# Four-layer graph network, one core: last pair columns split between two paths, a later clear, weights prepared earlier, one vector product per output tile

## The chip, the cores and the metric

The kernel runs on one core of a Trainium2 chip. The metric is the device time of one execution, in microseconds. The core has five engines that run their own instruction streams and wait for each other with semaphores: TensorE (PE, matrix products into PSUM), VectorE (DVE), ScalarE (ACT, activations and copies), GpSimd (POOL, here mostly indirect DMAs) and SyncE (SP, DMAs).

## What is computed

N = 1250 nodes with D = 512 features, E = 40000 edges sorted by `dst`. Four layers, each added to `x` and normalised by row. The first three need sums over edges, which the kernel writes as products with dense adjacency matrices; the last one (a SchNet-like filter network) needs an own product for every edge. Cut to what matters:

```python
def residual_norm(x, f):                  # _layernorm(x + f(x)), eps 1e-5
    y = x + f; return (y - mean(y)) / sqrt(var(y) + eps)
# L0: h = x + segment_sum(x[src], dst);  relu(h @ W1 + b1) @ W2 + b2
# L1: twice: relu(h @ W_self + (segment_sum(h[src], dst) / max(deg, 1)) @ W_neigh + b)
# L2: relu(segment_sum((x @ W)[src] * edge_weight[:, None], dst) + bias)
# L3: idx_i = src, idx_j = dst, f_ij = edge_attr_20, rcut_ij = edge_weight, r_ij = edge_attr_3
xs = x[:, :C] @ (W_in2f_s / sqrt(C));  xv = einsum('nci,cf->nfi', x[:, C:], W_in2f_v) / sqrt(C)
h = shifted_softplus(f_ij @ Wf1 + bf1)
W = (h @ Wf2 + bf2) * rcut_ij[:, None]    # the filter of each edge
agg = segment_sum(messages(xs[idx_j], xv[idx_j], W, r_ij), idx_i)   # 8 blocks of 128 used
S = shifted_softplus(agg[:, :2*F] @ (W1_s / sqrt(2*F))) @ (W2_s / sqrt(C))
V = einsum('nmi,mc->nci', agg[:, 2*F:8*F].reshape(n, 2*F, 3), W1_v) / sqrt(2*F)
V = einsum('nci,cd->ndi', V, W2_v) / sqrt(C)
```

## The kernel before

**Stages, in order.** Each engine has one program written out in order; nothing is scheduled by a planner. The nodes are NT = 10 row tiles of 128 (the last has 98 rows). The edges are 125 partitions by EJ = 320 columns, in BLOCKS_J = 10 blocks of LJ = 32 columns.

1. *Sorting the edges by pair of tiles (0 to 387 us).* Every edge gets a place in a table of (source tile, target tile) pairs (PAIR), and later one in a table sorted by source tile (SRC). `places` and `split_places` on DVE compute the places from products of PE. Then the pair records reach the table on two paths. The columns of the blocks in `DMA_BLOCKS` (six of ten, 192 columns, `DMA_COLS`) are written to DRAM by POOL, one indirect DMA for each column (L529), and the whole table is read back at the end (`pair_sb`, SP L438, after `pair_scat`). The columns of the other four blocks (128, `PERM_COLS`) go through TensorE: `one_hots` on DVE (L1307 to L1311) and `scale` on ACT (L1031) make five one-hot operands of a column, and `permute` on PE (L744) adds five products into PSUM, which I call one column product. A ring of four operand sets joins the three engines. PE runs some column products between other work; what is left when the input layer `x_up` is done runs as one backlog, all but the last LAST = 16 of it before DVE clears a part of the adjacency area (L1400, L1321) and the last 16 behind that. At the end DVE clears one more piece (L1405) and adds the PSUM sums to the table that was read back (L1412).
2. *Adjacency matrices (387 to 695 us)*: 416 chunks, `blocks` on PE (L800, L801), added by DVE (L1432). At its end POOL starts the 320 columns of the SRC table (L543).
3. *Layers L0, L1, L2 (695 to 1273 us)*: dense products on PE. The last is `l2_agg`, whose ten tiles DVE turns into the new `x` (`residual`, L1468 to L1459) as they come.
4. *The way into L3 (1273 to 1304 us)*: PE transposes `x` (`l3_xT`, L856), multiplies it (`l3_z`, L863), ACT copies each tile (L1090) and stores it to DRAM in `z_table` (L1092, on ACT's own queue, behind a wait for the copy). DVE prepares the weights of L3 (L1548 to L1585) behind its last `residual` tile. POOL clears the sums `agg` (L618, 128 x 10240), splits the edge attributes of two groups (`split`, L571 to L577), and then gathers rows of `z_table` for four chunks (L594), before it makes the low half of the hidden layer (`hidden_lo`, L602). ACT loads its table of functions (L1170).
5. *The edge loop of L3 (1304 to 2234 us)*: 322 chunks of 128 edges in 93 groups.
6. *The end (2234 to 2284 us)*: for each row tile PE transposes the sums (`sums_T`, L961), multiplies them with the first weights (`mixed`: L970 for the scalar part, L972 for the vector part), and after an activation with the second ones (`outputs`, four products, L982). ACT copies the transposed sums (L1193), copies the vector part (L1205) and computes the softplus (L1207 to L1209). DVE finishes the softplus (`activated`, L1667), adds `x` (L1673, L1675) and takes mean and variance (L1677, L1678) in `finish`. After the last tile come one square root for all rows (ACT L1211), a reciprocal (L1687), ten normalisations on DVE (L1691) and ten stores on ACT's queue (L1214).

Memory is reused all the time: `agg` lies where the adjacency matrices were, so it can't be cleared before the last `l2_agg` product has read them; `identb`, an operand of `attrs_T` (L875), lies there too.

## Time and profile before

| | us |
|---|---|
| median of 3 runs | 2282.49 (2280.95 to 2283.18) |
| the profiled execution | 2285.5, its span 2283.7 |
| PE busy | 2048.1 (90% of the span) |
| DVE busy | 1549.3 (68%) |
| POOL busy | 1393.4 (61%) |
| ACT busy | 1122.1 (49%) |

The chain that ended last is 68% PE, 10% DVE and 10% POOL. So PE sets the pace on the whole, but not in every stage: the POOL part is all in the first 387 us, and the DVE and ACT parts are at the borders between stages. A share of busy time is an average over all of them; what an edit is worth is read in its own stage.

### The profile page before, as it was taken

The page shows a single profiled execution, that of the slowest core. Times are in us where ns is not written, and L with a number is a line of the kernel's source. Part 1 is how long each engine was busy: PE and PEld are TensorE (multiplying, and loading weights), DVE is VectorE, ACT ScalarE, POOL GpSimd, SP SyncE. Part 2 cuts the span into 40 slices and gives each one's busy share as a digit, 9 for nine tenths or more (in the row PEclk, how much of TensorE's full clock was granted, in tenths as well). Part 3 has the DMA queues.
Part 4 walks back from the last instruction along what each step waited for, and adds up shares of the span by engine and source line. Part 5 has one row for each costly group of instructions (what it writes and reads, how often), then busy time and mean ns, then how long its engine had stood idle before and what let it go on. Part 6 is the DMA issues. An engine that isn't in the chain of part 4 may idle for free.

```text
span 2283.7 us, 37069 instructions
## 1 busy us (share of the span) xinstructions
PE 2048.1 (90%) x7761; PEld 1159.7 (51%) x7761; DVE 1549.3 (68%) x4326; ACT 1122.1 (49%) x3234; POOL 1393.4 (61%) x1718
## 2 busy tenths in 40 slices
PE   4788794777889999999999799999999999999986
PEld 3444342555665555455444555555555555555545
DVE  8987666888885251111403588888888888888885
ACT  0476454777771010000010466666666666666654
POOL 1477886444446888888885466666666666666530
PEclk9698797777779999999999899999999999999999
DMA  5410321000002121121120233333333333333321
GB/s 193 158 16 3 88 69 17 0 0 0 0 0 65 39 44 20 21 62 20 29 54 12 78 98 98 98 100 100 99 100 98 98 98 98 99 99 101 93 67 46
DMA packets 75080, 147.01 MB, mean 64 GB/s; under 512 B 26829, under 2 KB 37570, under 8 KB 74631
## 3 DMA queue, kind: packets, MB, share of 16 engines
q0 software_dynamic: 44704, 95.66, 17.3%
q1 hardware_dynamic: 27356, 45.20, 6.0%
q10 hardware_dynamic: 2946, 5.28, 0.6%
q8 instruction: 33, 0.54, 0.1%
q14 instruction: 41, 0.34, 0.0%
HBM read 123.11 MB, written 22.40 MB: 64 GB/s over the span
## 4 chain that ended last, share of the span: by engine, by line
PE 68%; DVE 10%; POOL 10%; issue 7%; DMA 2%; DVEq 2%; ACT 2%; ACTq 0%; SPq 0%; POOLq 0%
PE ps L910 24%; PE ps L653 11%; POOL pair_table L529 10%; PE ps L672 9%; PE ps L848 4%; PE ps L893 3%; PE ps L895 3%; PE ps L894 3%; PE ps L896 3%; DVE adj_t L1432 2%; PE ps L801 2%; DVE adj_t L1232 1%; DVE dense L1418 1%; DVE dense L1419 1%; DMA pair_table<-dense 1%
## 5 line engine op out<-in xcount | busy, mean ns | idle before, releaser
L910 PE MATMUL ps<-adj_t 128*128 128x512 f32 x1288 | 615.2, 600 | 14.3 <-DVE adj_t L1641 14.3
L1124 ACT ACTIVATE adj_t<-adj_t 128x128 f32<-128x128 f32 x966 | 315.3, 389 | 211.6 <-DVE adj_t L1620 189.4
L594 POOL DMA_INDIRECT adj_t<-z_table,adj_t x322 | 313.3, 973 | 154.5 <-DVE adj_t L1630 68.5
L910 PEld LDWEIGHTS ps<-adj_t 128*128 128x128 f32 x1288 | 231.2, 189 | 249.8 <-issue 215.6
L529 POOL DMA_INDIRECT pair_table<-dense x192 | 236.2, 1230 | 131.2 <-issue 120.7
L543 POOL DMA_INDIRECT src_table<-st_two,src_rows x216 | 262.9, 1217 | 70.5 <-issue 65.2
L801 PE MATMUL ps<-dense 128*128 128x128 f32 x832 | 226.7, 385 | 0.0
L672 PE MATMUL ps<-wring,dense 128*128 128x512 f32 (+1 forms) x480 | 209.9, 599 | 4.6 <-issue 3.9
L1432 DVE TENSOR_TENSOR adj_t<-adj_t,ps 128x256 f32 x416 | 173.5, 417 | 53.4 <-PE ps L801 40.6
L893 PE MATMUL ps<-dense_r 128*128 128x512 f32 x322 | 200.3, 622 | 2.3 <-POOL dense_r L602 2.3
L602 POOL TENSOR_TENSOR dense_r<-adj_t,dense_r 128x512 fp32r<-128x512 f32 x81 | 104.6, 1291 | 156.1 <-ACT dense_r L1133 155.9
L800 PE MATMUL ps<-dense 128*128 128x128 bf16 x416 | 109.0, 262 | 84.6 <-ACT dense L1059 75.8
L1622 DVE TENSOR_TENSOR adj_t<-adj_t,ps 128x384 f32<-128x384 f32 x322 | 176.0, 547 | 0.0
L801 PEld LDWEIGHTS ps<-dense 128*128 128x128 f32 x832 | 174.6, 260 | 1.6
L555 POOL TENSOR_SCALAR dense<-iotab,dense 128x128 bf16<-128x128 bf16 x104 | 68.5, 658 | 173.9 <-PE ps L801 165.1
L653 PE MATMUL ps<-adj_t,xa 128*128 128x512 f32 (+1 forms) x480 | 170.0, 516 | 3.6 <-DVE adj_t L1432 3.6
L1058 ACT ACTIVATE dense<-dense 128x128 f32<-128x128 bf16 x416 | 126.8, 305 | 88.3 <-DVE dense L1419 75.3
L1059 ACT ACTIVATE dense<-dense 128x128 f32<-128x128 bf16 x416 | 160.4, 386 | 0.0
L1641 DVE TENSOR_TENSOR adj_t<-adj_t,ps 128x1024 f32 x93 | 113.6, 1221 | 62.0 <-PE ps L910 61.0
L1620 DVE TENSOR_TENSOR adj_t<-adj_t,ps 128x256 f32<-128x256 f32 x322 | 133.7, 415 | 30.4 <-PE ps L896 27.7
L744 PE MATMUL ps<-dense 125*128 125x416 bf16 x640 | 143.3, 368 | 10.7 <-ACT dense L1031 10.3
L672 PEld LDWEIGHTS ps<-wring,dense 128*128 128x128 f32 (+1 forms) x480 | 90.8, 190 | 121.5 <-issue 121.5
(276 smaller groups left out, 3835.1 us busy)
## 6 DMA issues: line engine op xcount, KB each, us to landing
src_table<-dense SPq DMA_DIRECT2D x8, 656.0 KB, 6.6
adj_t<-z_table,adj_t POOLq DMA_INDIRECT x322, 3.5
records<-dense SPq DMA_DIRECT2D x1, 5000.0 KB
adj_t<-src_table SPq DMA_DIRECT2D x73, 64.0 KB
adj_t<-zeros SPq DMA_DIRECT2D x1, 4576.0 KB
src_table<-st_two,src_rows POOLq DMA_INDIRECT x216
st_two<-records POOLq DMA_DIRECT2D x54, 62.5 KB
adj_t<-zeros SPq DMA_DIRECT2D x1, 3328.0 KB
```

The costliest lines, as they stand in the source:

```text
L529: g.indirect_dma_start(out=pair_table, out_offset=bass.IndirectOffsetOnAxis(ap=rows_i[PAIR][0:EP, j:j + 1].bitcast(u32), axis=0), in_=pair ...
L543: g.indirect_dma_start(out=src_table, out_offset=bass.IndirectOffsetOnAxis(ap=rows_i[SRC][0:EP, j:j + 1].bitcast(u32), axis=0), in_=st_rec ...
L594: g.indirect_dma_start(out=zg[:, s, c, :], out_offset=None, in_=z_table, in_offset=bass.IndirectOffsetOnAxis(ap=dsti[:, s, c:c + 1].bitcas ...
L653: last = mm(b[:, 0:w], feats[:, t, m * P:(m + 1) * P], adj[:, k_of, t * N + c0:t * N + c0 + w], start=t == 0, stop=t == NT - 1)
L672: last = mm(b[0:r, :], lhs[:, k, t * P:t * P + r], w[:, k, :], start=a == 0 and k == 0, stop=a == len(parts) - 1 and k == KT - 1)
L801: mm(bank[c][:, P:2 * P], sel_f[:, c, 0, :], sel_f[:, c, 1, :], start=True, stop=True).then_inc(blk_done, 1)
L893: mm(bW[c], h_hi[:, s, e], wf2_hi, start=True, stop=False)
L910: last = mm(bank[6 + h], oh[:, c, :], msg[:, c, h * D:(h + 1) * D], start=c == c0, stop=c == c0 + count - 1)
L1059: A(sel_f[:, c, 1, :], sel_b[:, c, 1, :], ACT.Copy, scale=dense[:, ds(n * PAIR_COLS + (PAIR_AT + 2), 1)]).then_inc(selw_ready, 1)
L1124: last = A(msg[:, c, (2 + k) * P:(3 + k) * P], msg[:, c, MSG:MSG + P], ACT.Copy, scale=side[:, s, c, C_Y - ATT + k:C_Y - ATT + k + 1])
L1432: v.tensor_tensor(a, a, bank[c][:, 0:2 * P].rearrange("p (k n) -> p k n", k=2), ALU.add).then_inc(blk_added, 1)
L1622: v.tensor_tensor(msg[:, c, 5 * P:8 * P].rearrange("p (a n) -> p a n", a=3), zg[:, s, c, P:4 * P].rearrange("p (a n) -> p a n", a=3), b[:, ...
```

## The change

Five things, all in the order of the engines' programs:

- **Pair columns.** The last block of columns (block 9, `SHARED`) is cut in two: 16 of its columns stay with the DMAs, 16 become column products. So POOL issues 176 indirect DMAs and not 192, and PE, ACT and DVE make 144 column products and not 128. `split_places` does both kinds of work for that block.
- **The way into L3.** POOL's clear of `agg` waits for the last `residual` tile, not for the last `l2_agg` product. DVE prepares the L3 weights before the `residual` tiles of `l2_agg`; only `identb` and one small clear stay behind them. SP stores the z tiles, not ACT. ACT loads its table before the z copies. Only two gathers stand ahead of the first `hidden_lo`, and two behind it.
- **The vector weights.** Two new products make W1_v times W2_v once, before the loop: PE transposes `w1v`, ACT copies it, PE multiplies it with W2_v, ACT copies the result over `w1v`.
- **The end, vector part.** `mixed` writes the vector part of the output directly, with six 128 x 128 products for a tile (the L972 products and three of the four L982 products go away), and ACT's copy L1205 goes away.
- **The end, normalisation.** Each tile is normalised and stored (by SP) as soon as it can be. For tiles 0 to 7 ACT makes a first guess of the inverse root with Ln and Exp, and POOL refines it with four small instructions; for the last two ACT takes the square root and DVE the reciprocal.

```diff
-DMA_COLS = [t * LJ + c for t in DMA_BLOCKS for c in range(LJ)]
-PERM_COLS = [j for j in range(EJ) if j // LJ not in DMA_BLOCKS]
+SHARED = BLOCKS_J - 1
+DMA_COLS = [t * LJ + c for t in DMA_BLOCKS for c in range(LJ // 2 if t == SHARED else LJ)]
+PERM_COLS = [j for j in range(EJ) if j not in DMA_COLS]
...
@@ SP
             load_group(0, 0)
             load_group(0, 1)
+            for t in range(NT):
+                sp_eng.wait_ge(done["l3_z"], t + 1)
+                sp_eng.dma_start(z_table[t * P:t * P + rows_of(t), :], xb[0:rows_of(t), t, :]).then_inc(z_out, 16)
...
+            for t in range(NT):
+                sp_eng.wait_ge(y_ready, t + 1)
+                sp_eng.dma_start(out[t * P:t * P + rows_of(t), :], xa[0:rows_of(t), t, :]).then_inc(out_done, 16)
...
@@ POOL
-            pool.wait_ge(full, first["l2_agg"] + NT)
+            pool.wait_ge(done["l2_agg"], NT)
             g.memset(agg, 0.0).then_inc(agg_zero, 1)
             split(0, 0)
             split(0, 1)
-            for c in range(GROUP):
-                gather(0, 0, c)
+            gather(0, 0, 0)
+            gather(0, 0, 1)
             hidden_lo(0, 0)
+            gather(0, 0, 2)
+            gather(0, 0, 3)
...
+            for t in range(NT - 2):
+                pool.wait_ge(guessed, t + 1)
+                r, w = rstd[:, t:t + 1], rtmp[:, t:t + 1]
+                link(g.tensor_tensor(w, r, r, ALU.mult))
+                link(g.tensor_tensor(w, w, stat[:, 1, t:t + 1], ALU.mult))
+                link(g.tensor_scalar(w, w, -0.5, 1.5, ALU.mult, ALU.add))
+                g.tensor_tensor(r, r, w, ALU.mult).then_inc(refined, 1)
...
@@ PE
             pe.wait_ge(l3w_ready, 2)
+            for k in range(2):
+                last = nc.tensor.transpose(bank[6][:, k * P:(k + 1) * P], w1v[:, k, :], ident[:, :])
+            last.then_inc(wT_done, 1)
             for s in range(2):
                 attrs_T(0, s)
                 filter_in(0, s)
+            pe.wait_ge(wT_copied, 1)
+            for k in range(2):
+                last = mm(bank[7][:, k * P:(k + 1) * P], w1vT[:, k, :], w2sv[:, 1, :], start=True, stop=True)
+            last.then_inc(w12_done, 1)
+            pe.wait_ge(w12_ready, 1)
             filter_out(0, 0, 0)
...
@@ PE, mixed and outputs
-                for k in range(2):
-                    last = mm(svbank[s][:, P:D], w1v[:, k, :], aT[:, s, 2 + 3 * k:5 + 3 * k, :].rearrange("p m n -> p (m n)"),
-                              start=k == 0, stop=k == 1)
                 last.then_inc(sv_done, 1)
+                if t >= 2:
+                    pe.wait_ge(o_read, t - 1)
+                for m in range(3):
+                    for k in range(2):
+                        last = mm(obank[s][:, (1 + m) * P:(2 + m) * P], aT[:, s, 2 + 3 * k + m, :], w1v[:, k, :], start=k == 0, stop=k == 1)
+                last.then_inc(v_done, 1)
...
-                for m in range(KT):
-                    last = mm(obank[s][:, m * P:(m + 1) * P], svT[:, s, m * P:(m + 1) * P], w2sv[:, 0 if m == 0 else 1, :], start=True, stop=True)
-                last.then_inc(o_done, 1)
+                mm(obank[s][:, 0:P], svT[:, s, :], w2sv[:, 0, :], start=True, stop=True).then_inc(o_done, 1)
...
@@ ACT
             copies_T("l3_xT")
+            nc.scalar.preload_act_table_set("natural_log_exp_and_others")
...
-                act.wait_ge(done["l3_z"], t + 1)
-                act.dma_start(z_table[t * P:t * P + r, :], xb[0:r, t, :]).then_inc(z_out, 16)
...
+            act.wait_ge(wT_done, 1)
+            A(w1vT, bank[6][:, 0:2 * P].rearrange("p (k n) -> p k n", k=2), ACT.Copy).then_inc(wT_copied, 1)
             attrs(0, 0)
             softplus_exp(0, 0)
             softplus_log(0, 0)
             attrs(0, 1)
+            act.wait_ge(w12_done, 1)
+            A(w1v, bank[7][:, 0:2 * P].rearrange("p (k n) -> p k n", k=2), ACT.Copy).then_inc(w12_ready, 1)
             hidden_hi(0, 0)
...
@@ ACT, the end
+            def root(t):
+                r = rows_of(t)
+                act.wait_ge(var_ready, 3 * NT + t + 1)
+                if t < NT - 2:
+                    link(A(rstd[0:r, t:t + 1], stat[0:r, 1, t:t + 1], ACT.Ln))
+                    A(rstd[0:r, t:t + 1], rstd[0:r, t:t + 1], ACT.Exp, scale=-0.5).then_inc(guessed, 1)
+                else:
+                    A(rstd[0:r, t:t + 1], stat[0:r, 1, t:t + 1], ACT.Sqrt).then_inc(std_ready, 1)
...
-                A(svT[:, s, P:D], sv[:, P:D], ACT.Copy).then_inc(act_sv, 1)
...
@@ DVE
-            residual("l2_agg", 64, relu=True)
...
-            link(v.tensor_copy(identb, ident[:, :]))
...
+            residual("l2_agg", 64, relu=True)
+            link(v.tensor_copy(identb, ident[:, :]))
             v.memset(stat, 1.0).then_inc(l3w_ready, 1)
...
@@ DVE, the end
+                v.tensor_scalar(stat[0:r, 1, t:t + 1], stat[0:r, 1, t:t + 1], EPS, None, ALU.add).then_inc(var_ready, 1)
+
+            def normalised(t):
+                r = rows_of(t)
+                y = xa[0:r, t, :]
+                if t < NT - 2:
+                    dve.wait_ge(refined, t + 1)
+                else:
+                    dve.wait_ge(std_ready, 3 * NT + t - (NT - 2) + 1)
+                    link(v.reciprocal(rstd[0:r, t:t + 1], rstd[0:r, t:t + 1]))
+                v.tensor_scalar(y, y, stat[0:r, 0, t:t + 1], rstd[0:r, t:t + 1], ALU.subtract, ALU.mult).then_inc(y_ready, 1)
...
                 finish(t)
...
+                if t:
+                    normalised(t - 1)
+            normalised(NT - 1)
```

What the diff doesn't show is where the work then stands on an engine. On PE, at the end of the first stage (`wring,adj_t` is the input layer, `ps<-dense` with 416 columns a fifth of a column product), before:

```order
L744 MATMUL ps<-dense 128x416 x5
L756 MATMUL ps<-ident,xa 128x98 x4
L744 MATMUL ps<-dense 128x416 x5
L767 MATMUL ps<-wring,adj_t 128x512 x4
L744 MATMUL ps<-dense 128x416 x10
L767 MATMUL ps<-wring,adj_t 98x512 x4
L744 MATMUL ps<-dense 128x416 x125
```

and now:

```order
L765 MATMUL ps<-dense 128x416 x5
L777 MATMUL ps<-ident,xa 128x98 x4
L765 MATMUL ps<-dense 128x416 x5
L788 MATMUL ps<-wring,adj_t 128x512 x4
L765 MATMUL ps<-dense 128x416 x10
L788 MATMUL ps<-wring,adj_t 98x512 x4
L765 MATMUL ps<-dense 128x416 x205
```

The column products between other work are the same; the backlog behind the input layer grows from 25 to 41.

On ACT, between the last z copy and the first hidden layer, before:

```order
L1090 ACTIVATE dense<-ps 98x512
L1092 DMA z_table<-dense 98x512
L1170 ACT_TABLE_LOAD
L1100 ACTIVATE adj_t<-ps 126x512
L1108 ACTIVATE adj_t<-ps 128x512
L1110 ACTIVATE adj_t<-adj_t 128x512
L1116 ACTIVATE adj_t<-adj_t,wring 128x512
L1100 ACTIVATE adj_t<-ps 126x512
L1133 ACTIVATE dense_r<-adj_t 128x512
```

and now:

```order
L1116 ACT_TABLE_LOAD
L1119 ACTIVATE dense<-ps 128x512 x9
L1119 ACTIVATE dense<-ps 98x512
L1198 ACTIVATE adj_t<-ps 128x256
L1127 ACTIVATE adj_t<-ps 126x512
L1135 ACTIVATE adj_t<-ps 128x512
L1137 ACTIVATE adj_t<-adj_t 128x512
L1143 ACTIVATE adj_t<-adj_t,wring 128x512
L1127 ACTIVATE adj_t<-ps 126x512
L1204 ACTIVATE wring<-ps 128x256
L1160 ACTIVATE dense_r<-adj_t 128x512
```

The stores and the table load are gone from between; the two copies of 128x256 (L1198, L1204) are new, and the second stands ahead of `hidden_hi` (L1160, before L1133).

On PE, one tile of the end, before:

```order
L961 MATMUL ps<-ident,adj_t 128x128 x8
L970 MATMUL ps<-adj_t,wring 128x128 x2
L972 MATMUL ps<-adj_t,wring 128x384 x2
L982 MATMUL ps<-wring,dense 128x128 x4
L961 MATMUL ps<-ident,adj_t 128x128 x8
```

and now:

```order
L990 MATMUL ps<-ident,adj_t 128x128 x8
L999 MATMUL ps<-adj_t,wring 128x128 x2
L1005 MATMUL ps<-wring,adj_t 128x128 x6
L1011 MATMUL ps<-wring,dense 128x128
L990 MATMUL ps<-ident,adj_t 128x128 x8
```

And on DVE, one tile of the end, before:

```order
L1667 SCALAR_TENSOR_TENSOR dense<-ps,adj_t 128x128
L1673 TENSOR_TENSOR xa<-ps,xa 128x128
L1675 TENSOR_TENSOR xa<-ps,xa 128x3x128
L1677 BN_STATS lnt<-xa 128x6
L1678 BN_AGGR ybuf<-lnt 128x2
```

and now:

```order
L1706 SCALAR_TENSOR_TENSOR dense<-ps,adj_t 128x128
L1712 TENSOR_TENSOR xa<-ps,xa 128x128
L1714 TENSOR_TENSOR xa<-ps,xa 128x3x128
L1716 BN_STATS lnt<-xa 128x6
L1717 BN_AGGR ybuf<-lnt 128x2
L1718 TENSOR_SCALAR ybuf<-ybuf 128x1
L1728 TENSOR_SCALAR xa<-xa,ybuf,dense 128x512
```

PE loses two long and three short products for six short ones; DVE gains two instructions, one of them as wide as a tile.

## Rows read from the trace of the kernel before

**Rows 1.** Chain that ended last, 378 to 390 us: start, us, what.
```profile
378.03 1.19 POOL pair_table L529
...
379.52 2.61 DMA pair_table<-dense
...
386.85 2.50 DVE dense L1412 x3
```

**Rows 2.** PE, 320 to 392 us: start, us, instructions, idle before and its releaser.
```profile
350.52 15.59 PE L744 MATMUL ps<-dense 125*128 125x416 bf16 x80 [9.32 <-ACT dense L1031]
```

**Rows 3.** L744 alone: length, PE busy (x), PEld busy (x), granted clock, DMA.
```profile
196.90:201.40 4.50, 3.63 (x10) 1.17 (x10) 0.50 0.11 8
...
355.00:366.00 11.00, 11.00 (x64) 5.97 (x61) 1.00 0.09 4
```

**Rows 4.** DVE, 350 to 392 us, columns as in Rows 2.
```profile
366.52 1.42 DVE L1405 MEMSET adj_t<- 128x1632 f32 x1 [2.58 <-PE ps L744]
```

**Rows 5.** DVE, 1170 to 1315 us.
```profile
1265.00 0.55 DVE L1459 TENSOR_SCALAR xa<-ybuf,lnt 128x512 f32<-128x512 f32 x1
1270.57 0.69 DVE L1468 TENSOR_TENSOR ybuf<-ps,shared 98x512 f32<-98x512 f32 x1 [5.02 <-PE ps L848]
...
1273.59 5.85 DVE L1459 TENSOR_SCALAR xa<-ybuf,lnt 98x512 f32<-98x512 f32 x1
...
1299.88 0.69 DVE L1595 SCALAR_TENSOR_TENSOR adj_t<-ps,adj_t 128x512 f32<-128x512 f32 x1 [9.63 <-ACT adj_t L1116]
```

**Rows 6.** POOL, 1170 to 1315 us.
```profile
1270.53 8.64 POOL L618 MEMSET adj_t<- 128x10240 f32 x1 [35.93 <-PE ps L848]
...
1283.33 0.19 POOL L588 CAST adj_t<-adj_t 128x4 int32<-128x4 f32 x1
1297.34 1.03 POOL L594 DMA_INDIRECT adj_t<-z_table,adj_t  x1 [13.82 <-DMA z_table<-dense]
...
1302.18 1.28 POOL L602 TENSOR_TENSOR dense_r<-adj_t,dense_r 128x512 fp32r<-128x512 f32 x1
```

**Rows 7.** PE, 1170 to 1315 us.
```profile
1279.50 2.62 PE L856 MATMUL ps<-ident,xa 128*128 128x128 f32 x12 [5.90 <-DVE xa L1459]
1281.91 10.65 PE L863 MATMUL ps<-wring,dense 128*128 128x128 f32 x80
...
1303.61 0.77 PE L893 MATMUL ps<-dense_r 128*128 128x512 f32 x1 [2.31 <-POOL dense_r L602]
```

**Rows 8.** PE alone: length, PE busy (x), granted clock, DMA.
```profile
1279.50:1284.00 4.50, 4.50 (x22) 0.50 0.00 0
```

**Rows 9.** Chain that ended last, 1293 to 1298 us: start, us, what.
```profile
1294.16 0.61 ACT dense L1090
...
1294.79 2.28 DMA z_table<-dense
```

**Rows 10.** ACT, 1170 to 1315 us.
```profile
1295.16 1.28 ACT L1170 ACT_TABLE_LOAD   x1 [0.40 <-ACT dense L1090]
```

**Rows 11.** PE, 2190 to 2284 us: one tile of the end.
```profile
2255.45 1.04 PE L961 MATMUL ps<-ident,adj_t 128*128 128x128 f32 x8
...
2256.77 1.46 PE L972 MATMUL ps<-adj_t,wring 128*128 128x384 f32 x4
2258.06 1.05 PE L982 MATMUL ps<-wring,dense 128*128 128x128 f32 x8
2258.95 1.04 PE L961 MATMUL ps<-ident,adj_t 128*128 128x128 f32 x8
```

**Rows 12.** DVE, 2190 to 2284 us.
```profile
2256.29 0.29 DVE L1667 SCALAR_TENSOR_TENSOR dense<-ps,adj_t 128x128 f32<-128x128 f32 x1 [1.31 <-ACT adj_t L1209]
...
2258.27 0.18 DVE L1678 BATCH_NORM_AGGREGATE ybuf<-lnt 128x2 f32<-128x6 f32 x1
...
2273.37 0.18 DVE L1678 BATCH_NORM_AGGREGATE ybuf<-lnt 98x2 f32<-98x6 f32 x1
```

**Rows 13.** ACT's DMA issues, 2274 to 2284 us.
```profile
2274.87 5.88 ACTq L1214 DMA_DIRECT2D out_x<-xa  x10
```

47 lines of the change are left out of this document (21 added, 26 removed).

## The prediction, made before the changed kernel was run

> **What bounds the kernel now.** I read the chain that ended last first, since it says for each stage which engine's end was waited for, and then the instructions in order of time at the borders between stages, since all edits lie there. The long dense products (695 to 1273 us) and the edge loop (1304 to 2234 us) are PE's and are not touched. Three places are.
>
> *The front, up to 387 us.* The reader sees in [rows 1] that the chain runs through POOL: the last indirect DMA starts at 379.52, 1.49 behind the one before, has landed at 382.13, and once the table has been read back DVE adds the sums at 386.85. The other path is done long before: PE's column products end at 366.11 [rows 2], DVE's last clear at 367.94 [rows 4]. So POOL's path is 18.9 us later than PE's.
>
> *The way into L3.* At 1273.59 DVE's normalisation of the last tile takes 5.85 us where the tile before took 0.55 [rows 5]. It ends at 1279.44; POOL's clear, 8.64 us from 1270.53, ends at 1279.17 [rows 6]. PE stands still for 5.90 us, released by that instruction [rows 7], and its granted clock then is 0.50, the lower of its two levels, until 1284 [rows 8]. The first gather waits until the last z tile has been stored, 1297.07 [rows 6, 9], and the first filter product until POOL has made the low half, 1303.61 [rows 6, 7].
>
> *The end.* PE is busy without a gap: a tile takes 3.50 us (2255.45 to 2258.95), of which 1.32 are transposes and scalar product, 1.29 the long vector products, 0.89 the four output products [rows 11]. From DVE's last statistics (2273.55 [rows 12]) to the end of the span, 2283.7, come another 10.15 us: root, ten normalisations and ten stores, whose issue ends at 2280.75, 2.95 before the end [rows 13].
>
> **The change part by part.** The sums are made against the profiled execution (2285.5, span 2283.7). It is 3.0 above the median of the runs; I carry the difference over to the median.
>
> *Front.* POOL saves 16 DMAs at 1.49 us, 23.9 us: its last issue and the read-back are that much earlier, so DVE could add the sums at 363. The other path gets 16 more column products, all of them in the backlog behind the input layer, where nothing hides them. A product's price: at full clock 64 fifths take 11.0 us, 0.86 us a product [rows 3]; in the whole last run, with its slow start, 80 take 15.59, 0.97 us [rows 2]. I take 0.92, in the middle, since the slow start is there only once: 14.8 us, between 13.8 and 15.6. The products end at 380.9; DVE's clear starts 0.41 behind them as now and takes 1.42 [rows 4]; the sums are added at 382.7 in place of 386.85. **Gain 4.1 us**, 3.3 to 5.1. What is late next is PE's path itself, so each us on it counts from now on. The three extra small instructions of `split_places` I cost at nothing, since DVE then waits for PE's bases of the source tables; uncovered they are 1 us.
>
> *The way into L3.* With the clear behind the last `residual`, the normalisation takes 0.55 and PE goes on at 1274.25. The weight preparation, 10.8 us (from 1279.44 to 9.63 before 1299.88 [rows 5]), now runs while PE works on `l2_agg`; DVE waits 5.02 us for PE before a tile there [rows 5], so it has caught up after two or three tiles: nothing. PE: twelve transposes take 2.62 at clock 0.50 [rows 7, 8] and half of that, 1.3, at full clock, which there is no pause to take away. A z tile then costs what eight records of the same shape cost in the end stage, 0.89 [rows 11], ten of them 8.9 in place of 10.65 [rows 7]. PE ends at 1284.6. ACT's copies (0.61 [rows 9]) follow PE without stores between them; the table load (1.28 [rows 10]) lies in the wait for the first z tile. Last copy done at 1285.2, stored 2.28 later at 1287.5, gather 0.28 behind, at 1287.8. POOL: clear from 1274.25 to 1282.9, then two splits and small copies, 4.35 as before (1279.17 to 1283.52 [rows 6]): ready at 1287.3. So the gather comes 9.5 earlier, and POOL, only 0.5 behind the store, is late next.
>
> The hidden layer's path: `attrs_T` starts 0.3 after the last copy, behind two transposes of w1v, at 1285.5. Before, it followed the last copy (1294.77) too, but ACT's next step stood behind the table load until 1296.44, some 0.8 longer than it had to [rows 9, 10]. So the hidden layer is ready about 1290.3 in place of 1300.57 [rows 5]. Now ACT's `hidden_hi` stands behind the copy of the combined weights, and that behind the second `filter_in`, which waits for the hidden layer itself: 0.7 for this product (0.77 for one as wide at half clock, L893 [rows 7]), 0.4 to 0.9 for two products of four records (0.11 each [rows 11], twice that at half clock), 0.4 to 0.6 for the copy. No row has this wait; the least is 0, if the copy falls into a pause, the most 2.5. I take 2.0, near the sum of its links. Then 0.6 for `hidden_hi`, POOL's low half (1.28 [rows 6]) from 1292.9 to 1294.2, and the first filter product at 1294.3 in place of 1303.61. **Gain 9.3 us**, 6 to 11.5. The two gathers moved behind the low half are issued by 1296.8 and needed by DVE about 1300. Loop and dense stages stay as they are.
>
> The 5.85 us have a rule of the Trainium skill beside them: SBUF — State Buffer, section Who interferes with whom, says that VectorE and GpSimd share a pair of ports as a lock, and whoever starts first holds it for its whole instruction. By that rule the cast of `identb`, now right behind the last `residual`, may wait for the clear to end at 1282.9; PE asks for it at 1285.3, so it would delay nothing, with 2.4 us to spare.
>
> *The end.* PE: six short products at 0.22 (0.89/4 [rows 11]) cost 1.34 for the 1.29 of the long ones, and one output product in place of four saves 0.67: 2.88 us a tile, 0.62 less. DVE: a tile's work from L1667 to the end of L1678 is 2.16 us [rows 12]; it gains the sum with epsilon (about as long as L1678, 0.2) and a normalisation (0.55 [rows 5]), with their starts 3.0. So DVE becomes the bound, at about 3.05 us a tile. Following both engines tile by tile with these prices (for the old order this gives the traced 2273.55), the last statistics come 3.1 us earlier. Then root, reciprocal and small steps, 0.77 (2273.55 to the first normalisation, which ends where the first store is issued, 2274.87 [rows 12, 13]), the last normalisation 0.55, 0.2 for tile 8's in between, an issue of 0.6 (5.88/10), and a landing between 1.9 (the z store behind its own issue) and 2.95: 4.5 us in place of 10.15. Together 8.7. From it I take 0.5 for DVE held up by POOL's four small instructions a tile; no row shows that pair, the bounds are 0 and 3 us. **Gain 8.2 us**, 5.5 to 9.5.
>
> *Sum*: 4.1 + 9.3 + 8.2 = 21.6. The profiled execution would take 2263.9, the median 2282.5 - 21.6 = **2261 us**.
>
> **The rivals.**
>
> *A, POOL holds the way into L3*: the splits run slower beside DVE, or the combined weights cost more, and only the stalled 5.3 us come back; the end gives 5.5. 4.1 + 5.3 + 5.5 = 14.9: 2267.6. For it: POOL is 0.5 us from being the bound, and DVE takes work in both places. Against: the same splits took 4.35 beside a busy DVE.
>
> *B, the front gives nothing*: at 1.18 us a column product (18.9/16) PE's path is as late as POOL's was: 2265. For it: ACT and DVE feed each product, beside POOL's DMAs. Against: 0.86 to 0.97 so far.
>
> *C, slower: the backlog at the lower clock.* At granted clock 0.50 two products hold 3.63 us, 1.73 to 1.82 each [rows 3]. The backlog is 41 long; it starts at 333 (nine products of 0.9 before the pause that begins at 341.2 [rows 2]), holds that pause of 9.3 and ends 1.8 before the sums: they are added at 344 + 41p. With the other gains of 17.5 the kernel is slower than before once 344 + 41p passes 404.4, from 1.47 us a product on. At 1.73 the sums come 28 late: 2293. For it: the clock does fall in this stage. Against: 1.00 from 355 to 366, once PE was busy.
>
> *D, another chain is as late*, and within 0.2% comes out, 2280. For it only that the chain shows one path of several; against it three plain waits of 18.9, 5.9 and 10.15 us, each on the chain.
>
> *E, more*: 2253, with free combined weights and a short landing.
>
> **How the numbers follow.** The forecast has 0.58, A 0.18, B 0.12, E 0.05, D 0.04, C 0.03. The likeliest is 2261. Its terms' bounds give gains of 14.8 to 26.1, so 2256 to 2268, with A and B inside; I widen to 2254 and 2270, which leaves D, C and part of E out. 0.2% is 4.6 us, about what a measurement of this kernel can tell from no change. Faster by more: forecast, A, B and E, 0.93, of which I give 0.01 away: 0.92. Within: D, 0.04. Slower: C and 0.01 unnamed, 0.04.
>
> **What would show it.** Front: the last indirect DMA at 355 to 357 us, the column products ending at 380 to 382, the sums added within 2.5 us of that; wrong if they come after 384, C if the products' run shows clock 0.50. Way into L3: the last normalisation 0.55, a pause of PE under 1 us, clock 1.00 through the z tiles, the gather 13 to 14 us after PE resumes and the first filter product 20 us after it (24.1 before). End: a tile every 3.05 us, DVE without pauses and PE with some, and 4.5 us from the last statistics to the end. The prediction is wrong if DVE waits there for POOL or ACT, or if the loop, which I leave alone, grows.

## The result, and the profile after

The changed kernel takes 2246.4 us in the median of four runs (2246.0 to 2248.2), where the kernel before, timed beside it, takes 2282.7. The ratio is 0.984, with a 95% interval of 0.983 to 0.986. That is 36 us faster; the forecast was 21.6, and 2246.4 lies below its range (2254 to 2270). The two profiled executions differ by about as much: spans of 2283.7 and 2246.0 us, 37.7 apart. Two of the runs that were timed later fell far outside all others, one of the kernel before at 4051.6 us and one of the changed kernel at 2672.6, and no ratio below holds them.

The span is cut into five stretches at the same events in both traces: the sums added by DVE, the last product of `l2_agg` on PE (its pause starts there), the first filter product, the end of the last product of the edge loop, the end.

| stretch | before | after | gain | forecast |
|---|---|---|---|---|
| start to sums added | 386.85 | 363.24 | 23.6 | 4.1 |
| sums added to the last product of l2_agg | 886.8 | 886.8 | 0 | 0 |
| from there to the first filter product | 30.0 | 20.6 | 9.4 | 9.3 |
| edge loop | 928.8 | 932.3 | -3.5 | 0 |
| last product of the loop to the end | 51.3 | 43.1 | 8.2 | 8.2 |
| span | 2283.7 | 2246.0 | 37.7 | 21.6 |

Two rows are off: the front gave 19.5 us more than forecast, and the edge loop, which the change leaves alone, grew by 3.5 us.

**The front.** The chain that ended last, 354 to 366 us of the changed kernel (start, us, what), answers to [rows 1]:

```profile
354.66 1.19 POOL pair_table L540
356.15 2.60 DMA pair_table<-dense
358.83 4.29 DMA dense<-pair_table
363.24 2.54 DVE dense L1449 x3
```

POOL is still the bound: its last indirect DMA starts at 356.15 in place of 379.52, 16 times 1.46 us sooner. The forecast had PE's path behind it. In the changed kernel's timeline (start, us, instructions, idle before and its releaser) the last run of column products on PE, then DVE's last clear, as in [rows 2, 4]:

```profile
328.71 16.45 PE L765 MATMUL ps<-dense 125*128 125x416 bf16 x80 [9.38 <-ACT dense L1059]
```

```profile
345.57 1.42 DVE L1442 MEMSET adj_t<- 128x1632 f32 x1 [2.72 <-PE ps L765]
```

The products end at 345.2, not at 380.9. With 16 more of them the path is 21 us *earlier* than before (366.1). DVE's last clear is done at 347.0, 16 us before the sums can be added.

**The way into L3.** PE, then POOL, of the changed kernel, 1250 to 1271 us, answering to [rows 6, 7]:

```profile
1250.60 1.55 PE L877 MATMUL ps<-ident,xa 128*128 128x128 f32 x12 [0.59 <-DVE xa L1496]
1251.99 9.10 PE L884 MATMUL ps<-wring,dense 128*128 128x128 f32 x80
...
1266.99 1.06 PE L966 MATMUL ps<-wring,adj_t 128*128 128x128 f32 x4
1270.58 0.77 PE L914 MATMUL ps<-dense_r 128*128 128x512 f32 x1 [2.53 <-POOL dense_r L613]
```

```profile
1250.61 8.65 POOL L629 MEMSET adj_t<- 128x10240 f32 x1 [43.48 <-DVE xa L1496]
1265.67 1.02 POOL L605 DMA_INDIRECT adj_t<-z_table,adj_t  x1 [2.37 <-DMA z_table<-dense]
...
1269.17 1.26 POOL L613 TENSOR_TENSOR dense_r<-adj_t,dense_r 128x512 fp32r<-128x512 f32 x1 [1.22 <-ACT dense_r L1160]
```

PE's pause is 0.59 us where it was 5.90; twelve transposes take 1.55 and the 80 z products 9.1 (forecast 1.3 and 8.9), at a granted clock of 1.00 (1250 to 1262 us). The gather is released by the stored z table, as before, and POOL waits 2.37 for it: rival A, POOL as the bound, did not come.

**The end.** One tile of the changed kernel on PE, then three rows of DVE, answering to [rows 11, 12]:

```profile
2220.63 1.04 PE L990 MATMUL ps<-ident,adj_t 128*128 128x128 f32 x8
2221.50 0.61 PE L999 MATMUL ps<-adj_t,wring 128*128 128x128 f32 x4
2221.95 1.56 PE L1005 MATMUL ps<-wring,adj_t 128*128 128x128 f32 x12
2223.35 0.39 PE L1011 MATMUL ps<-wring,dense 128*128 128x128 f32 x2
2223.57 1.04 PE L990 MATMUL ps<-ident,adj_t 128*128 128x128 f32 x8
```

```profile
2223.76 0.29 DVE L1706 SCALAR_TENSOR_TENSOR dense<-ps,adj_t 128x128 f32<-128x128 f32 x1 [0.32 <-ACT adj_t L1246]
...
2240.14 0.18 DVE L1717 BATCH_NORM_AGGREGATE ybuf<-lnt 98x2 f32<-98x6 f32 x1
...
2241.28 0.55 DVE L1728 TENSOR_SCALAR xa<-xa,ybuf,dense 98x512 f32<-98x512 f32 x1
```

This tile takes 2.94 us (2220.63 to 2223.57), the next 3.13; ten of them put the last statistics at 2240.3, and the span ends 5.7 us behind. At every second tile in the middle of the end DVE waits 0.31 to 0.34 us for ACT's softplus (the first DVE row), which the prediction had named as a sign of being wrong; in the kernel before it was 1.31 in the tile shown [rows 12].

### The profile page after: what moved, and what is told of

Read it like the earlier page. It is cut to its first block, busy times and chain, and to the rows that moved or that the text cites. A ratio compares the mean times of both kernels' runs of the same rounds, so it can differ in the third digit from the quotient of the medians.

```text
span 2246.0 us, 37456 instructions
## 1 busy us (share of the span) xinstructions
PE 2039.9 (91%) x7867; PEld 1155.7 (51%) x7867; DVE 1557.0 (69%) x4403; ACT 1131.7 (50%) x3291; POOL 1374.2 (61%) x1734
## 4 chain that ended last, share of the span: by engine, by line
PE 69%; DVE 10%; POOL 9%; issue 6%; DMA 2%; DVEq 2%; ACT 1%; ACTq 0%; SPq 0%; POOLq 0%
PE ps L931 25%; PE ps L674 11%; PE ps L693 9%; POOL pair_table L540 9%; PE ps L869 4%; PE ps L914 3%; PE ps L916 3%; PE ps L915 3%; PE ps L917 3%; DVE adj_t L1469 3%; PE ps L822 2%; DVE adj_t L1267 2%; DVE dense L1455 1%; DVE dense L1456 1%; DMA pair_table<-dense 1%
## 5 line engine op out<-in xcount | busy, mean ns | idle before, releaser
L540 POOL DMA_INDIRECT pair_table<-dense x176 | 218.2, 1240 | 125.9 <-issue 115.1
L822 PE MATMUL ps<-dense 128*128 128x128 f32 x832 | 221.6, 377 | 0.0
L822 PEld LDWEIGHTS ps<-dense 128*128 128x128 f32 x832 | 170.1, 253 | 1.6
L1059 ACT ACTIVATE dense<-dense,adj_t 125x128 bf16<-125x128 bf16 x432 | 136.8, 387 | 54.1 <-DVE dense L1344 53.5
L1678 DVE TENSOR_TENSOR adj_t<-adj_t,ps 128x1024 f32 x93 | 113.6, 1221 | 66.7 <-PE ps L931 65.6
L765 PE MATMUL ps<-dense 125*128 125x416 bf16 x720 | 149.6, 352 | 11.0 <-ACT dense L1059 10.1
```

The costliest lines, as they stand in the source:

```text
L540: g.indirect_dma_start(out=pair_table, out_offset=bass.IndirectOffsetOnAxis(ap=rows_i[PAIR][0:EP, j:j + 1].bitcast(u32), axis=0), in_=pair ...
L822: mm(bank[c][:, P:2 * P], sel_f[:, c, 0, :], sel_f[:, c, 1, :], start=True, stop=True).then_inc(blk_done, 1)
```

## The experiments

There are fifteen runs. The first question is the front: is the fast path of PE something that the change brings about, or was the first trace of the kernel before unusual?

### Both kernels again

> The kernel before, unchanged, in a second profiled execution. In the first one the column products ended at 366.1 us (L744, 350.52 + 15.59), far from the 386.85 at which the sums were added, and the granted clock fell to 0.57 at 140-150 us and 0.66 at 170-180 us; in the changed kernel, with the same instructions on PE, DVE and ACT up to 203 us, the clock stood at 1.00 from 110 to 200 us and that stretch ran 38 us faster. Theory 'state': how fast the placing stage runs differs from one execution to the next, since PE, DVE and ACT wait for each other there and the clock falls when PE has pauses; then this second execution may end its products at another time (by over 3 us from 366.1), with the total time the same, 2282 within 4 us, since POOL's DMAs set the end of the front. Theory 'kernel': it is a property of the program as built; then the products end at 366 within 1 us and the clock falls at the same places.

> The changed kernel, unchanged, in a second profiled execution. Its first one ended the column products at 345.2 us and added the sums at 363.2. Theory 'state': the products may end anywhere between 345 and 381 us (366.1 of the kernel before and 16 more columns at 0.92), and the total stays at 2246 to 2249 as long as they end by 361; above that it grows with them, to 2266 at 381. Theory 'kernel': the products end at 345 within 1 us and the total is 2246 to 2249.

Nothing is edited in either. The kernel before took 2283.2 us, as always, and its products ended at 331.5 instead of 366.1. PE of this second execution:

```profile
314.58 16.92 PE L744 MATMUL ps<-dense 125*128 125x416 bf16 x80 [9.25 <-ACT dense L1031]
```

The 35 us arise between 110 and 243 us, where DVE works out places, ACT scales and PE forms one column product a step. SP's first clear (L415) waits for the block offsets, which are worked out behind that stage, so its start follows the stage's end. Its row in the first, then in the second execution of the kernel before:

```profile
243.05 0.37 SPq L415 DMA_DIRECT2D adj_t<-zeros  x1
```

```profile
204.59 0.37 SPq L415 DMA_DIRECT2D adj_t<-zeros  x1
```

PE alone in stretches of 20 us (length, PE busy (x), granted clock, DMA share, GB/s), first and second execution of the same program:

```profile
110.00:130.00 20.00, 18.09 (x117) 1.00 0.28 66
130.00:150.00 20.00, 17.25 (x82) 0.74 0.09 3
150.00:170.00 20.00, 17.36 (x107) 1.00 0.09 3
170.00:190.00 20.00, 16.86 (x90) 0.83 0.09 3
190.00:210.00 20.00, 15.90 (x80) 0.83 0.09 4
```

```profile
110.00:130.00 20.00, 19.68 (x131) 1.00 0.26 64
130.00:150.00 20.00, 18.15 (x119) 1.00 0.10 4
150.00:170.00 20.00, 18.66 (x123) 1.00 0.09 3
170.00:190.00 20.00, 17.80 (x117) 1.00 0.09 4
```

From 130 to 150 us PE does 82 instructions in the first execution and 119 in the second; the granted clock is 0.74, a mean of the two levels, and 1.00. The clock is not all of it. From 110 to 230 us these rows put some 31 us at the lower level (with 0.83 from 210 to 230 too); a step takes 2.77 us there (PE's L716 at 144.14 and 146.91) and 1.50 at full clock, so an estimate from these numbers is that the clock costs about 14 of the 38 us. The rest is pace, and it begins at full clock, before the clock falls. DVE's first instruction of a step, 117 to 120 us, in the first execution and in the second:

```profile
117.53 0.57 DVE L1278 TENSOR_TENSOR dense<-ps,adj_t 125x400 f32<-125x400 f32 x1 [0.66 <-PE ps L719]
119.78 0.57 DVE L1278 TENSOR_TENSOR adj_t<-ps,adj_t 125x400 f32<-125x400 f32 x1 [0.68 <-PE ps L719]
```

```profile
115.79 0.56 DVE L1278 TENSOR_TENSOR dense<-ps,adj_t 125x400 f32<-125x400 f32 x1
117.29 0.56 DVE L1278 TENSOR_TENSOR adj_t<-ps,adj_t 125x400 f32<-125x400 f32 x1
```

A step takes 2.25 us with a wait of DVE for PE, or 1.50 us without one, at the same clock. The first execution has steps of both kinds: from 100 us on, 22 of its 39 steps at full clock take over 2 us, where the second execution has 7 such steps of 57. The changed kernel's second execution took 2244.8 us, its products ended at 343.7, its sums were added at 361.5. So the theory "state" holds: the same program ran this stage at two speeds, and the speed belongs to the execution. What set it is not shown.

### The sharing alone, and everything but the sharing

> The kernel before with the sharing of the last block alone: 16 of its 32 pair columns go to the products, the rest is unchanged. Theory: POOL's chain of scatters ends 16 x 1.49 = 23.8 us earlier and stays the bound, so the time falls by 23.6 to 23.8 us, to about 2259 (ratio 0.9896). Rival 'products': the path of PE ends at 381 as forecast, the time falls by 4 us only, to 2278 (0.998), and the rest of the 36 us comes from the other edits. Rival 'kernel': the fast placing stage belongs to the other edits of the changed kernel, so that the products end at 381 here.

> The changed kernel with the sharing undone: all 32 columns of the last block are scattered by POOL again, everything else of the change stays. Theory: sums added at 386.9 again, the time is 2246.4 + 23.7 = 2270.1 (ratio to before 0.9945: the way into layer 3 9.4 and the end 8.2, less 3.6 to 4 that the edge loop takes longer). Rival 'products' (the sharing gives 4): 2250.5, ratio 0.986.

```diff
-DMA_COLS = [t * LJ + c for t in DMA_BLOCKS for c in range(LJ)]
-PERM_COLS = [j for j in range(EJ) if j // LJ not in DMA_BLOCKS]
+SHARED = BLOCKS_J - 1
+DMA_COLS = [t * LJ + c for t in DMA_BLOCKS for c in range(LJ // 2 if t == SHARED else LJ)]
+PERM_COLS = [j for j in range(EJ) if j not in DMA_COLS]
```

(with the second branch in `split_places`, as in the change's diff; added to the kernel before, and taken out of the changed one). DVE adds the sums, with the sharing alone (from the chain that ended last) and without it (DVE's timeline):

```profile
362.79 2.51 DVE dense L1415 x3
```

```profile
386.27 2.49 DVE L1446 SCALAR_TENSOR_TENSOR dense<-dense,ps 128x416 f32<-128x416 f32 x3 [55.00 <-DMA dense<-pair_table]
```

The sharing moves the sums by 23.3 to 23.5 us. The products end at 343.1 with it and at 329.4 without: 13.7 for 16 columns, 0.86 each, just below the 13.8 to 15.6 of the forecast (in these two executions SP's clear started at 203.2, so their placing stages ended together). But the time is 2264.4 us with the sharing alone (ratio 0.9915, interval 0.9898 to 0.9932), 19.4 below the 2283.8 before and not 23.7; without it 2266.9 (0.9924, 0.9907 to 0.9940), not 2270.1. The missing 4 us are in the edge loop: 932.7 us in x3, which has the sharing, 928.3 in x4, which doesn't. The three executions without the sharing up to then needed 928 to 929, the three with it 932 to 933. Nothing that the sharing edits runs in that loop.

### Where a loop stands in DVE's program

One turn of the edge loop takes 22.71 us with the sharing and 22.60 without it. Two additions of the sums fall into a turn. In the changed kernel (its third execution, x12 below) and in the one with 61 more DVE instructions (x5), DVE's rows of three successive additions, one turn from the first to the third (L1678; L1680 in x5), are:

```profile
1704.62 1.22 DVE L1678 TENSOR_TENSOR adj_t<-adj_t,ps 128x1024 f32 x1 [0.71 <-PE ps L931]
1715.99 1.22 DVE L1678 TENSOR_TENSOR adj_t<-adj_t,ps 128x1024 f32 x1 [0.73 <-PE ps L931]
1727.32 1.22 DVE L1678 TENSOR_TENSOR adj_t<-adj_t,ps 128x1024 f32 x1 [0.71 <-PE ps L931]
```

```profile
1711.06 1.22 DVE L1680 TENSOR_TENSOR adj_t<-adj_t,ps 128x1024 f32 x1 [0.61 <-PE ps L931]
1722.41 1.22 DVE L1680 TENSOR_TENSOR adj_t<-adj_t,ps 128x1024 f32 x1 [0.70 <-PE ps L931]
1733.66 1.22 DVE L1680 TENSOR_TENSOR adj_t<-adj_t,ps 128x1024 f32 x1 [0.62 <-PE ps L931]
```

In the slow loop both additions come about 0.7 us behind DVE's instruction before; in the fast one, one of the two comes 0.61 behind. In x3 and x4, laid over each other from the same filter product on, PE starts the products waited for 1.40 and 1.41 us into the turn, and DVE's addition comes at 3.73 and 3.64. Ahead of each addition DVE loads a register (the slot's offset) and works out an address. So the program text on DVE was the suspect, by elimination: the sharing adds 67 DVE instructions ahead of the loop, whose first one is number 1366 in DVE's program without it and 1433 with it. (The traces, where earlier loops count once for every turn, have 2190 and 2257 DVE instructions ahead of the first addition, the same 67 apart.)

> The changed kernel, with one DVE memset (L1442, 1632 columns) cut into 62 short ones: 61 more DVE instructions ahead of the edge loop, in a stretch where DVE waits 16 us for POOL. Background: with the sharing (two executions of the changed kernel and the kernel with the sharing alone) one turn of the edge loop takes 22.71 us, without it (two executions of the kernel before and the changed kernel without sharing) 22.60, 33 turns or so long; within a turn the difference of 0.09 arises on DVE ahead of its addition of the sums (L1678), where nothing of the change stands. Theory 'place': DVE's loop starts at its instruction 1366 in the fast ones and 1433 in the slow ones, and what comes in late there is DVE's code; with 61 more it starts at 1494 = 1366 + 128, and a turn takes 22.60 again, the time falls by 3.6 us to a ratio of 0.983 to before. Rival 'another engine or the data': a turn stays at 22.71, the ratio at 0.9844 to 0.985.

> The kernel before with 67 more DVE instructions in the same place (L1405 cut into 68): DVE's edge loop starts at its instruction 1433, as in the changed kernel, and nothing else differs. Theory 'place': a turn of the edge loop takes 22.71 us in place of 22.60, and the time rises by 3.6 us (ratio 1.0016). Rival 'another engine or the data': 22.60, ratio 1.000.

```diff
-            v.memset(adj_t[:, LATE_AT:2 * AW_COLS], 0.0).then_inc(adj_zero, 1)
-            dve.wait_ge(adj_zero, 1)
+            cuts = [LATE_AT + (2 * AW_COLS - LATE_AT) * k // 62 for k in range(63)]
+            for a, b in zip(cuts, cuts[1:]):
+                v.memset(adj_t[:, a:b], 0.0).then_inc(adj_zero, 1)
+            dve.wait_ge(adj_zero, 62)
```

(68 pieces in the kernel before). Both came out: 22.60 us a turn and a loop of 927.5 for the changed kernel with 61 more instructions, 22.72 and 933.7 for the kernel before with 67 more. The times are 2239.4 us (0.9809, 0.9793 to 0.9826) and 2287.6 (1.0018, 1.0009 to 1.0028); expected were 0.983 and 1.0016. The loop's part is 4.8 and 4.9, more than 33 times 0.11, since the first turn and the groups ahead of it differ too. That DVE's position decides is shown, from both sides; why 1433 is bad is not. One rival can be put aside: the queues that carry the program's own code (kind "instruction" in the profile) moved no packet between 1350 and 2050 us, in the slow loops (the changed kernel, x6) or in the fast one (x5), so, as far as these queues show, the 0.11 us are not code that is fetched anew in every turn. The other kernels give more positions: 1366, 1370, 1382, 1465, 1494 and 1497 are fast, 1433 is slow in each of the seven executions that had it (932 to 934 us).

### More columns by products

> The changed kernel with 8 of the last block's columns scattered and 24 by products (16 and 16 in the changed one). POOL's chain ends 8 x 1.49 = 11.9 us earlier, at sums 351.3; the products end 8 x 0.86 = 6.9 us later, at 351 to 352, with the memset behind them 354. Theory: the two paths meet, sums at 351 to 354, the time falls by 9 to 11 us against the changed kernel, to a ratio of about 0.980. If a slow placing stage (as in the first execution of the kernel before, 35 us later) comes up, that execution is 20 us or more longer, since the products then set the end; runs that agree within 3 us say that it is rare. Rival 'products' as forecast (0.92 a column from 381): the time rises by 25 us.

> The changed kernel with none of the last block's columns scattered and all 32 by products. POOL's chain ends 23.8 us earlier than in the changed kernel (339.4), the products 16 x 0.86 = 13.8 later (358 to 359, memset 361). Theory: the products are now the bound, sums at 360 to 361, time 2 to 3 us below the changed kernel and 7 to 8 above that with 8 columns scattered (ratio 0.983), and the times of the executions now show how even the placing stage is: a slow one would be 30 us longer. Rival: with the placing stage's speed of the first trace of before, the sums come at 396 and the time rises by 33 us.

```diff
-DMA_COLS = [t * LJ + c for t in DMA_BLOCKS for c in range(LJ // 2 if t == SHARED else LJ)]
+DMA_COLS = [t * LJ + c for t in DMA_BLOCKS for c in range(8 if t == SHARED else LJ)]
-        PAIR_SCATTERED = 16 * len(DMA_COLS) // 2
+        PAIR_SCATTERED = [16 * sum((q // BURST) % 2 == k for q in range(len(DMA_COLS))) for k in range(2)]
-                        sp_eng.wait_ge(pair_scat[k], PAIR_SCATTERED)
+                        sp_eng.wait_ge(pair_scat[k], PAIR_SCATTERED[k])
```

(0 in place of 8 in the second). PE, then DVE, of the kernel with 8 scattered:

```profile
343.29 16.53 PE L765 MATMUL ps<-dense 125*128 125x416 bf16 x80 [9.95 <-DVE dense L1348]
```

```profile
360.23 1.42 DVE L1442 MEMSET adj_t<- 128x1632 f32 x1 [2.95 <-PE ps L765]
361.68 2.49 DVE L1449 SCALAR_TENSOR_TENSOR dense<-dense,ps 128x416 f32<-128x416 f32 x3
```

Now the sums follow straight behind DVE's clear: the products are the bound, as the prediction had it for 16 columns, and POOL has issued its last DMA at 342.4. But no 9 to 11 us were gained at the sums (361.7, and 363.7 with none scattered). The four kernels of that chip had SP's clear at 212 to 216 us, where the eight of two other chips (x1 to x4, x9 to x12) had 203 to 206. So the products ended 8 us later than worked out from those (359.8 with 8 scattered, for 351 to 352; 361.9 with none, for 358 to 359). The times, 2244.0 us (0.9832) and 2244.9 (0.9836), hold another gain that is not the front's: their loops took 927.9 and 927.5, since 32 and 64 more DVE instructions had moved it. The fair measure for them is x5, on the same chip, with 16 scattered and a fast loop of 927.5: its 2239.4 us are 4.6 and 5.4 less. So more products than 16 columns gained nothing and, if anything, lost. The four executions with none scattered spread over 6.9 us (2239.6 to 2246.5), those of x5 over 0.7; that fits a bound whose stage before it is uneven, but only one execution of each was profiled.

### What a pause does to the placing stage

> The kernel before with one delay on DVE in the placing stage: at step 30 of 80 the reduction L1281 is repeated four times, about 3 us in which PE and ACT wait once. Theory 'pace': PE's pauses and the lower granted clock keep each other up; one pause of 3 us is enough to bring the clock down once, and the stage (203 to 206 us at SP's clear in most executions, 243 in the first of the kernel before) ends by more than the 3 us later, 8 to 40. Rival 'one pause is only itself': the clear starts at 207 to 210, with the clock at 0.97 or more from 110 to 200 us. The time stays at 2283 either way, since POOL sets the front's end.

> The kernel before with eight delays on DVE in the placing stage, two more reductions (about 1.4 us) at each of eight steps, 11 us in all. Theory 'pace': the clock falls in several of them, as in the first execution of the kernel before (0.57 at 140-150, 0.66 at 170-180, 0.67 at 210-220), and the stage ends 20 to 40 us later, at 225 to 245. Rival: the delays only add up, the clear starts at 214 to 218, the clock stays above 0.97.

> The kernel before, unchanged, a third profiled execution, beside the two with delays. Thirteen later executions with the same instructions up to there had the clear at 203 to 216 us; I expect 203 to 216 again and the column products at 331 to 341 us. If it comes at 243, the slow stage is frequent.

```diff
+                for k in range(4 if s == PAIR and n == 30 else 0):
+                    link(v.tensor_reduce(pos_f[:, n * L:(n + 1) * L], pv.rearrange("p (a b) -> p a b", b=B), AX.X, ALU.add))
                 v.tensor_reduce(pos_f[:, n * L:(n + 1) * L], pv.rearrange("p (a b) -> p a b", b=B), AX.X, ALU.add).then_inc(pos_step[s], 1)
```

(in the other, two repetitions at n = 21, 29, ... 77). The one delay held DVE for 2.4 us, and PE stood still for 1.46 before it went on at 119.7. PE in stretches of 4 us (columns as above):

```profile
116.00:120.00 4.00, 2.54 (x17) 1.00 0.41 118
120.00:124.00 4.00, 3.76 (x17) 0.54 0.14 3
124.00:128.00 4.00, 4.00 (x19) 0.61 0.10 4
128.00:132.00 4.00, 4.00 (x29) 1.00 0.06 2
```

The granted clock was back at 1.00 by 128, and the clear started at 213.4: not later than in the unchanged kernel on the same chip, 215.1. Eight delays of 1.21 us each: 220.7, which is 5.6 later for 9.7 us of delays.

```profile
220.66 0.37 SPq L415 DMA_DIRECT2D adj_t<-zeros  x1
```

So the theory "pace" did not come out: the pause brought the clock down for a moment and it recovered, and neither execution (one of each kernel) was thrown into the slow form. What did so in the first execution of the kernel before, and in none of the sixteen others (203 to 221 us), **stays open**.

### The way into L3 and the end, taken apart

> The changed kernel once more, timed on the same chip as the other three: 2244 to 2248 us, a turn of the edge loop 22.71 us; the column products end at 343 to 355 and the sums are added at 361.5 to 363.3, set by POOL.

It took 2247.7 us (0.9839, 0.9826 to 0.9852), sums added at 362.3, loop 932.5. It is the measure for the next three, run on the same chip.

> The changed kernel with the end as before (long vector products, four output products a tile, root, normalisations and ACT's stores behind the last tile) and without the combined weights; front and way into layer 3 as changed. Theory: from the last product of the edge loop's sums to the end of the span 51.3 us as before in place of 43.1, so 8.2 more; the way into layer 3 without the combined weights 1.2 to 2 less; together 6.2 to 7 us above the changed kernel. Rival 'the end gives more or less': the stretch differs from 51.3 by over 1 us, or the loop's length from 932, so that the gain of the end was partly that of another edit.

(the change's diff taken back in the end stage and for the combined weights). 2254.8 us, 7.1 more. The end takes 51.3 us again, 8.2 more; from the last product of `l2_agg` to the first filter product 19.4 in place of 20.6, so the combined weights cost 1.2 us there; the loop is unchanged. (The times are 7.1 apart, as 8.2 less 1.2 has it; the two profiled spans 8.4, since the front came 1.3 later.)

> The changed kernel with POOL's clear of the sums started as before, once PE has ended l2_agg, in place of behind DVE's last normalisation; all else as changed. Theory: the last normalisation takes 5.9 us again in place of 0.55, PE pauses and resumes at the lower granted clock, and the first filter product comes 5.3 (the stall) to 7 us (with transposes and z products at the lower clock) later, the time likewise, ratio to the changed kernel 1.0024 to 1.003. Rival 'POOL is as late': the clear, started 3 us earlier, lets POOL's splits end earlier, so that only 2 us are lost.

```diff
-            pool.wait_ge(done["l2_agg"], NT)
+            pool.wait_ge(full, first["l2_agg"] + NT)
```

2255.8 us, 8.1 more. PE has its pause again:

```profile
1255.58 2.62 PE L877 MATMUL ps<-ident,xa 128*128 128x128 f32 x12 [5.90 <-DVE xa L1496]
```

The same stretch takes 27.8 us in place of 20.6: 5.3 for the stall and 2.0 more, transposes and z products at the lower granted clock, just above the 5.3 to 7 that were expected. So 7.3 of the 9.4 us of this term are the place of the clear. (The two spans differ by 7.8: these 7.3 and a front 3.9 later, less 3.1 in the dense stages and 0.3 in the loop.) The trace says what stood beside what: the clear ran from 1246.62 to 1255.25, and the normalisation, started at 1249.68, ended 0.3 us behind it. DVE's instructions just ahead of it ran beside the same clear and kept their times (0.69 us for the last `BATCH_NORM_STATS2`), so only this one was held. The Trainium skill, page SBUF — State Buffer, section Who interferes with whom, has the two engines share one pair of ports as a lock, which the instruction that took it first keeps to its end, and says that not every DVE instruction needs the pair. This run agrees with it: with the clear alone moved, the normalisation goes from 0.55 to 5.9 us.

> The changed kernel with DVE's clear cut into 62 pieces (as in the run with 61 more instructions) and ACT's copy of the combined weights moved behind hidden_hi, PE's wait for it behind the first two filter groups. Theory: a turn of the edge loop takes 22.60 us, and hidden_hi starts 1.9 us earlier; POOL then makes the low half behind its second gather, so the first filter product comes 1.2 us earlier than with the pieces alone. Time: changed kernel less 4.7 (loop, as measured between the two) less 1.2, about 2240. Rival: the combined weights' copy was hidden anyway, nothing comes of the 1.2.

```diff
+            hidden_hi(0, 0)
             act.wait_ge(w12_done, 1)
             A(w1v, bank[7][:, 0:2 * P].rearrange("p (k n) -> p k n", k=2), ACT.Copy).then_inc(w12_ready, 1)
-            hidden_hi(0, 0)
```

(on top of x5; PE's wait for `w12_ready` moved behind the two calls of `filter_out`). PE's first filter product:

```profile
1267.42 0.77 PE L914 MATMUL ps<-dense_r 128*128 128x512 f32 x1 [1.89 <-POOL dense_r L613]
```

It comes 19.4 us behind the last product of `l2_agg`, 1.2 sooner, all that the combined weights had cost. With the loop at 927.8 the kernel takes 2239.3 us (0.9802, 0.9789 to 0.9814), 8.4 below the changed kernel beside it; this is the fastest of all, if only by what separates it from x5 (0.9809), which these runs cannot resolve. Of the 6.7 between the two profiled spans, 4.7 are the loop, 1.2 the weights, and 2.1 the dense stages, less 1.3 of a later front. The dense stages took 883 to 887 us from one execution to the next; why is open.

## Why the prediction was wrong

*The direction and three of five stretches were right; the front was not.* The step that failed is "the other path gets 16 more column products ... the products end at 380.9". Its price of a column held: 0.86 us measured (x3 against x4), 0.92 taken. Its starting point did not. 366.1, the end of the products in [rows 2], was read as a property of the kernel. It was that of one execution, in which an earlier stage had ended 37 to 40 us later than in nine of the sixteen others, and 22 to 31 later than in the other seven. With the 331.5 of the second execution, the same working gives 331.5 + 14.8 = 346.3 for the products (345.2 came) and leaves POOL's path, "DVE could add the sums at 363", as the bound (363.24 came). The 340 and 341 of two other chips (x6, x13, x15) give 355 to 356, still ahead of POOL. The sum would then have been 23.9 + 9.3 + 8.2 = 41.4; the spans came 37.7 apart, and nearly all that is missing is the 3.5 of the loop. Why the first execution was slow there stays open; that it was not the kernel is what x1 and x15 show.

The trace could have warned. The path was 19 us off the chain, so the time, 2280.5 to 2285.5 us in the runs of the kernel before, said nothing of it: a path with that much slack may be 35 us shorter in the next execution and nobody sees it. And its own rows were uneven: column products at granted clocks of 0.50 and 1.00 [rows 3], which the forecast used for a price but not as a sign that the stage before them might run otherwise. Rival C had the stage's unevenness, on the slow side only.

*Rivals.* B and C put PE's path even later and fell with it. A fell: POOL waited 2.37 us for the z table. D fell: the time moved by 36 us. E was right in sign, for another reason than its own, and its 2253 is still too high.

*The way into L3*, 9.3 forecast, 9.4 measured. The 30.0 us before are the longest of seven executions with the old order (28.8 to 30.0), and seven with the new one took 20.3 to 20.6: the gain lies between 8.2 and 9.7. Its largest part, the stall and the lower clock behind it, is 7.3 (x10). The wait of the combined weights, "I take 2.0", was 1.9 on ACT, from the hidden layer (1266.47) to `hidden_hi` (1268.37), but only 1.2 on the path (x9, x11), since POOL's second gather filled the rest. The cast of `identb`, which the prediction had perhaps waiting for the clear, took 0.22 us at 1250.46, ahead of the clear's start at 1250.61.

*The end*, 8.2 forecast, 8.2 measured, and x9 gives the same. Two errors cancel. The last statistics came 3.7 us earlier, where 3.1 less 0.5 for POOL's small instructions was forecast: DVE has no wait for POOL in the middle of the end (2208 to 2238 us). Nor is DVE the clear bound that the prediction made it: it waits 0.3 us for ACT at every second tile, and the chain that ended last runs through PE there; the two tiles above take 3.03 us on average all the same, where 3.05 was forecast. The last steps took 5.7 us where 4.5 was forecast, since the landing was longer, from the end of the last store's issue at 2242.2 to 2246.0.

*The loop*, "which I leave alone", grew by 3.5 us: 0.35 in the first turn and 0.11 in each of 32 more, less 0.3 in the groups ahead of them. The prediction put this term at nothing ("Loop and dense stages stay as they are") and named its growth as a sign that it was wrong, but priced no way in which an edit elsewhere could reach it. The 67 more DVE instructions ahead of the loop are that way (x5, x6).

## What to carry to other kernels

A path beside the critical one has no witness in the times. Before a sum moves the bound onto it, its length needs a second execution, or a range as wide as its unevenest stage; the critical path's own number (here 363) is the safer end. Where two paths with different resources share work, balance them by measured ends over several executions, not by one trace: here 16 columns on each side were at least as good as 24 or 32 for the products. With 16, the products ended anywhere from 343 to 354 us (and would have ended near 381 in an execution as slow as the first), while POOL's last DMA started at 354 to 359. And after any edit ahead of a hardware loop, compare the length of one turn, not only the stretch that was edited.

## What the runs showed of the hardware that was not expected

- The same loop, with the same instructions, takes 22.60 or 22.71 us a turn depending on how many DVE instructions stand ahead of it in the program: first instruction 1366, 1370, 1382, 1465, 1494 or 1497 fast, 1433 slow. Sixty-one more short instructions, placed where DVE waits, take 4.8 us off the changed kernel's loop (ratio of the whole 0.981 for 0.984). Why is open.
- Three engines that hand each other one column at a time run a step in 1.50 us or in 2.25, at the same granted clock, and how many steps are of the long kind differs from one execution to the next (22 of 39, 7 of 57); the stage's end was at 203 to 206 us on two chips, 212 to 216 on two others, and once at 243.
- After one pause of PE of 1.5 us the mean granted clock was 0.54 and 0.61 in the next two stretches of 4 us, and 1.00 behind them; the stage ended no later for it. Eight delays of 9.7 us together cost 5.6.
